# A chunk's residual sum and norm taken in four separate items; key norms kept aside, gate logits scaled once per event, last gates' functions one item later

## What is computed

```python
x = _layernorm(x + _L0_ffn_ref(x, ...))            # the end of the routed feed-forward
q = _rmsnorm((x @ Wq).reshape(B, T, H, D), q_rms_w) # H = 16, D = 64
k = _rmsnorm((x @ Wk).reshape(B, T, H, D), k_rms_w)
v = (x @ Wv).reshape(B, T, H, D)
gate = softplus(einsum('bthd,hd->bht', k, u_n) / sqrt(D))
bias = -dist * omega_eff * gate                     # per key and head
scores = einsum('bihd,bjhd->bhij', q, k) / sqrt(D) + bias
```

## Time and profile before

| | us |
|---|---|
| median of three runs (lowest to highest) | 2246.51 (2245.86 to 2251.53) |
| profiled execution, device time | 2246.59 |
| profiled execution, span from first to last instruction | 2244.8 |
| PE busy | 2050.4 (91% of the span) |
| DVE busy | 1368.2 (61%) |
| ACT busy | 1151.4 (51%) |
| POOL busy | 843.5 (38%) |
| mean granted TensorE clock | 0.953 of 2.4 GHz |

### The profile page before, as it was taken

One profiled execution on the slowest core, in us unless ns is written; L12 is line 12 of the kernel. 1 busy time (PEld: TensorE's weight loads), 2 busy tenths in 40 slices (PEclk: granted clock), 3 DMA queues, 4 the chain that ended last, 5 costly groups with the idle time before them and its releaser, 6 DMA issues.

```text
span 2244.8 us, 34359 instructions
## 1 busy us (share of the span) xinstructions
PE 2050.4 (91%) x11728; PEld 1168.5 (52%) x11728; DVE 1368.2 (61%) x3345; ACT 1151.4 (51%) x1859; POOL 843.5 (38%) x544
## 2 busy tenths in 40 slices
PE   5799999998496888796999999999999999999998
PEld 2333333334395454453565656556665655655644
DVE  4788888884532878774666666666666654333311
ACT  2366666666353677673455555555555553223232
POOL 5000000001502345342677777777777773000000
PEclk8799999999598999995999999999999999999999
DMA  5233333113174779877577667776777687533300
GB/s 179 98 127 131 131 128 119 59 51 112 62 202 123 219 232 333 251 240 185 139 179 176 157 163 178 176 172 154 171 178 179 158 218 198 129 89 85 90 5 10
DMA packets 260300, 335.88 MB, mean 150 GB/s; under 512 B 22732, under 2 KB 181756, under 8 KB 259720
## 3 DMA queue, kind: packets, MB, share of 16 engines
q1 hardware_dynamic: 244824, 305.82, 50.6%
q0 software_dynamic: 7664, 24.39, 3.0%
q10 hardware_dynamic: 7640, 3.48, 0.5%
HBM read 193.69 MB, written 122.62 MB: 141 GB/s over the span
## 4 chain that ended last, share of the span: by engine, by line
PE 40%; issue 6%; DVE 4%; SPq 2%; DMA 1%; ACT 0%; DVEq 0%
PE ps L1287 10%; PE ps L956 6%; PE ps L940 6%; PE ps L909 6%; PE ps L941 5%; PE ps L1238 2%; DVE a1mx L1012 2%; PE ps L1298 1%; PE ps L1275 1%; PE ps L1276 1%; PE ps L943 1%; DVE a1mx L1008 1%; SPq L1162 1%; DMA a1FQ<-s_q 0%; DVE a1mx L1005 0%
## 5 line engine op out<-in xcount | busy, mean ns | idle before, releaser
L1123 POOL TENSOR_TENSOR a1sum<-a1sum,a1prob 128x1024 f32<-128x1024 f32 (+3 forms) x256 | 462.9, 1808 | 82.6 <-ACT a1prob L1066 50.5
L1066 ACT ACTIVATE a1prob<-ps 128x512 f32<-128x512 f32 (+2 forms) x640 | 328.0, 554 | 243.6 <-PE ps L943 211.9
L479 DVE TENSOR_REDUCE a0grid<-ps 128x8 f32<-128x1024 f32 x288 | 351.3, 1223 | 100.6 <-PE ps L351 63.1
L1005 DVE CUSTOM_DVE_ANT_0 ps<-ps,c_mask_ij 128x128 f32<-128x128 f32 x496 | 264.4, 551 | 193.9 <-issue 189.7
L580 ACT ACTIVATE a0prob<-ps 128x1024 f32<-128x1024 f32 x288 | 286.2, 1024 | 167.3 <-PE ps L377 110.5
L940 PE MATMUL ps<-a1QA,a1KA 69*128 69x512 f32 (+3 forms) x768 | 284.3, 378 | 4.6 <-DMA a1QA<-a1neg 4.6
L956 PE MATMUL ps<-a1prob,a1V 128*64 128x512 f32 (+3 forms) x1536 | 272.9, 498 | 3.9 <-ACT a1prob L1066 3.9
L941 PE MATMUL ps<-a1QB,a1KB 128*128 128x512 f32 (+3 forms) x768 | 263.1, 350 | 0.0
L909 PE MATMUL ps<-a1KA,a1QA 68*128 68x128 f32 x744 | 224.6, 381 | 4.3 <-DMA a1KA<-s_g 3.4
L956 PEld LDWEIGHTS ps<-a1prob,a1V 128*64 128x64 f32 x1536 | 102.7, 138 | 171.6 <-issue 138.1
L1008 DVE TENSOR_REDUCE a1mx<-ps 128x1 f32<-128x320 f32 x248 | 146.0, 589 | 70.1 <-PE ps L909 67.2
(11 more groups left out here) (267 smaller groups left out, 3163.1 us busy)
## 6 DMA issues: line engine op xcount, KB each, us to landing
a1FQ<-s_q SPq DMA_DIRECT2D x128, 256.0 KB, 7.9
a1KB<-s_k SPq DMA_DIRECT2D x128, 256.0 KB, 8.6
s_xs<-c_zero POOLq DMA_DIRECT2D x19, 1024.0 KB, 9.5
s_q<-mqkT SPq DMA_DIRECT2D x32, 512.0 KB, 4.4
s_v<-mv SPq DMA_DIRECT2D x32, 512.0 KB, 5.8
s_k<-a1KH SPq DMA_DIRECT2D x32, 512.0 KB, 4.9
s_k<-a1KL SPq DMA_DIRECT2D x32, 512.0 KB, 5.9
a1KA<-s_k SPq DMA_DIRECT2D x64, 256.0 KB
```

What stands on the lines that cost most here:

```text
L479: dve.tensor_reduce(grid[g % 2][:, :, a:b + 1:b - a], banks(("max", k)), axis=AX.X, op=ALU.max).then_inc(s1_free, 1)
L1005: dve.tensor_tensor_reduce(bank[:, 0:w], bank[:, 0:w], const["mask_ij"][:, BANK - w:BANK], 1.0, LOWEST, ALU.add, ALU.max, mx[:, x % 2, h, ...
L1066: act.activation(weights_of(g, u)[:, group[0]:group[-1] + 1, off:BANK], both(e, u, group), ACT.Exp).then_inc(weighed, 1)
L1123: pool.tensor_tensor(t[:, :, off:BANK], t[:, :, off:BANK], weights_of(g, u)[:, :, off:BANK], ALU.add).then_inc(summed, 1)
```

## The change

`join` is taken apart into `add_up` (the sum), `count` (bn_stats) and `moments` (bn_aggr). For a chunk c + 2 the sum now stands in item 8 and the statistics in item 11 of chunk c; the moments follow in item 2 and the norm in item 5 of chunk c + 1. Chunk 1 has sum, statistics and moments in item 2 of chunk 0. In `scale` the reciprocal of a key's norm is written to a new tensor `kss`, kept for all chunks, and no longer multiplied into `z` there; `gates_a` multiplies the event's whole `z` by it in one instruction, and waits for that. `count` waits for the statistics' earlier reading, `moments` for the norm before. On ScalarE the last event's `soften` moves from n = 96 to n = 97, behind the weighing of the last keys.

```diff
@@ -1498,7 +1498,8 @@
         EVENTS = {24: range(0, 2), 72: range(2, 6), 96: range(6, 8)}
         wide = TILES * max(len(cs) for cs in EVENTS.values())
         zabs, g, gj = own("zabs", [P, wide, heads]), own("g", [P, wide, heads]), own("gj", [P, wide, heads])
-        z = own("z", [P, steps, TILES, heads])
+
+        z, kss = own("z", [P, steps, TILES, heads]), own("kss", [P, steps, TILES, heads])
         aug, augT = own("aug", [P, wide, P // heads, heads], F32R), [own(f"augT{r}", [4 * heads, CHUNK]) for r in range(2)]
         warm = own("warm", [P, 1])
         tmp = sq[0]
@@ -2194,18 +2195,26 @@
 
             dve = nc.vector
 
-            def join(c):
+            def add_up(c):
 
                 dve.wait_ge(gathered[c % 2], 16 * TILES * (c // 2 + 1))
                 if c > 1:
                     dve.wait_ge(x2_full, c - 1)
                 dve.scalar_tensor_tensor(acc[c % 2][:, :, :], x1[:, c * TILES:(c + 1) * TILES, :], 2.0, yg[c % 2][:, :, :], ALU.mult, ALU.add).then_inc(added, 1)
+
+            def count(c):
+
                 dve.wait_ge(added, c + 1)
                 if c > 0:
-                    dve.wait_ge(x2_full, c)
+                    dve.wait_ge(counted2, 2 * c * TILES)
                 for t in range(TILES):
                     dve.bn_stats(st2[:, t, :], acc[c % 2][:, t, :]).then_inc(counted2, 1)
+
+            def moments(c):
+
                 dve.wait_ge(counted2, (2 * c + 1) * TILES)
+                if c > 0:
+                    dve.wait_ge(x2_full, c)
                 for t in range(TILES):
                     dve.bn_aggr(mv2[:, t, :], st2[:, t, :]).then_inc(counted2, 1)
 
@@ -2234,17 +2243,15 @@
                 (tile, kind), i = kinds(n), nth(n)
                 c, t = divmod(tile, TILES)
                 dve.wait_ge(rooted3, i + 1)
-                dve.reciprocal(ss[i % 2][:, :], ss[i % 2][:, :]).then_inc(ss_full, 1)
+                norms = kss[:, c, t, :] if kind == WK else ss[i % 2][:, :]
+                dve.reciprocal(norms, ss[i % 2][:, :]).then_inc(ss_full, 1)
                 dve.wait_ge(ss_full, i + 1)
                 if i >= 3:
                     a = n // 3 * 3 + kind
                     old = [m for m in range(n) if kinds(m)[1] != WV][-3]
                     dve.wait_ge(t_full, at["half", old, 1] + 1)
-                if kind == WK:
-                    dve.wait_ge(z_full, c + 1)
-                    dve.tensor_tensor(z[:, c, t, :], z[:, c, t, :], ss[i % 2][:, :], ALU.mult).then_inc(z_scaled, 1)
                 dve.tensor_tensor(qk[i % 3][:, :].rearrange("p (h d) -> p h d", d=dim), pair(n).rearrange("p (h d) -> p h d", d=dim),
-                                  ss[i % 2][:, :].unsqueeze(2).to_broadcast([P, heads, dim]), ALU.mult).then_inc(scaled, 1)
+                                  norms.unsqueeze(2).to_broadcast([P, heads, dim]), ALU.mult).then_inc(scaled, 1)
 
             def parts(k):
 
@@ -2255,7 +2262,11 @@
             def gates_a(k):
 
                 n, zs, za, _, _ = parts(k)
-                dve.wait_ge(z_scaled, (events[k][-1] + 1) * TILES)
+                cs = events[k]
+                dve.wait_ge(z_full, cs[-1] + 1)
+                dve.wait_ge(ss_full, 2 * TILES * (cs[-1] + 1))
+                dve.tensor_tensor(zs, zs, kss[:, cs[0]:cs[-1] + 1, :, :].rearrange("p c t h -> p (c t) h"), ALU.mult).then_inc(z_scaled, 1)
+                dve.wait_ge(z_scaled, k + 1)
                 if k > 0:
                     dve.wait_ge(gated, GSTEP * k)
                 dve.scalar_tensor_tensor(za, zs, -1.0, zs, ALU.mult, ALU.max).then_inc(gated, 1)
@@ -2314,16 +2325,23 @@
 
             GSTEP = 8
             dve.wait_ge(made, PREPARED)
-            join(0)
-            norm(0)
+            for part in (add_up, count, moments, norm):
+                part(0)
             for n in range(NI + TLAG):
                 if 1 <= n <= NI and kinds(n - 1)[1] != WV:
                     scale(n - 1)
                 if n < NI and kinds(n)[1] != WV:
                     reduce(n)
                 c, o = divmod(n, 12)
+                if n == 2:
+                    add_up(1)
+                    count(1)
                 if o == 2 and c + 1 < steps:
-                    join(c + 1)
+                    moments(c + 1)
+                if o == 8 and c + 2 < steps:
+                    add_up(c + 2)
+                if o == 11 and c + 2 < steps:
+                    count(c + 2)
                 if o == 5 and c + 1 < steps:
                     norm(c + 1)
                 if n in EVENTS:
@@ -2437,8 +2455,9 @@
                     keep_x(c + 1)
                 if o == 11 and c + 1 < steps:
                     keep_z(c + 1)
-                if n in EVENTS:
-                    soften(event_of[EVENTS[n][0]])
+                for m, cs in EVENTS.items():
+                    if n == m + (cs[-1] == steps - 1):
+                        soften(event_of[cs[0]])
                 if n in split_at:
                     split(split_at.index(n))
                 for c in turn_gates.get(n, ()):
```

## The result

The changed kernel takes 2221.6 us in the median (2219.41 to 2230.44) beside 2246.9 (2245.86 to 2252.29) of the kernel before on the same chip: a ratio of 0.9885, 95% interval 0.9856 to 0.9914, 25.3 us less. The profiled execution took 2221.2 us, its span is 2219.4. The forecast was 2229, with a range of 2212 to 2241.

A forecast was written before the change was run, and what follows sets the result against it. VectorE's order of work, with z held behind GpSimd's subtraction, was taken as the bound. Terms 1.6 + 1.1 + 2.5 + 0 + 6.6 + 2.5 + 2.9 = 17.2 us off 2246.59 gave 2229.4, range 2212 to 2241.

The forecast's parts named there:

- Bound and mechanism: Middle stage's last part: VectorE's order of work sets the time; PE waits 32.6 us for mqk, holding costs z 25 us.
- Norm held: Item 5: GpSimd's subtraction holds the norm's tensor_scalar, costing PE 3.0 us per plain chunk; likeliest case, 2229 us, chance 0.48.
- X: Time by which a moved VectorE part ends after mqk of the keys; 4.3 us for the held norm.
- the prediction's rule: Value items: a part ending X us after mqk of the keys costs PE X - 1.2, leaving 0.4 of lateness.
- the floor: TensorE's minimum for a chunk of twelve items without idle gaps: 29.0 us.
- Add_up and count: Items 8 and 11: the sum, held by a subtraction, costs PE 0.6 us; the unheld bn_stats cost 0.2.
- the slack of 0.4: Value items, read from an undisturbed tile: 0.4 us more beyond VectorE's 0.8 us of idle before PE is late.
- Clock: Plain chunks: half of the half-clock loss seen behind 2.37 us of PE idling, charged at 0.9 us per chunk.
- a plain chunk: Norm 3.0, add_up 0.6, count 0.2 and clock 0.9 put such a chunk 4.7 us over the floor.
- no gain: Chunks 3 and 4: 10.8 us over the floor now, 2 x 4.7 then, each lower about 1.2 us more.
- handed back elsewhere: Rival: the gain is lost to DMA limits in chunks 2 to 5 or GpSimd behind key stores; 2245 us, chance 0.09.
- End of the stage: Weighing the last keys before the gates' functions moves everything up to the barrier 2.9 us earlier.

The follow-up runs named there:

- z alone: Kernel before with only the key norms kept aside and z multiplied once per event, join whole in item 2: ratio 0.9912, 17.4 us less in the medians.
- the join alone: Kernel before with only the join split into four items, z left in place: ratio 0.9969, 5.9 us less in the medians.
- functions back: Changed kernel with the last event's soften at n = 96 again: chunks unchanged, first maximum 8.30 us behind the last item's product.
- the last version: Changed kernel with norm in item 6, gathers one per tile, fifteen next-stage loads issued later: 2217.25 us beside 2230.32 of the changed kernel.

## Why the prediction was right, and where it was not

*Bound and mechanism.* Right: VectorE's order set this part outside chunks 3 and 4, and the holds on z were the largest piece. In the chunks z alone gives 15.3 us, the join alone 4.9, and both together ("functions back") 19.9. That the single gains add up is chance: in chunk 5 they make 13.5 where both together give 8.4, and in chunks 3 and 4 they lengthen by 4.5 and 2.3 where both together lengthen by 2.3.

*Norm held.* The mechanism was right, in chunks 1, 3 and 5 with 2.4 to 2.5 us; chunks 0 and 4 saw 1.0, chunks 2 and 6 none. The Trainium skill, "SBUF — State Buffer", section "Who interferes with whom", says of the shared pair of ports that "whoever issues first gets the shared pair for the whole instruction; the other **fully blocks**"; the trace agrees, down to the first of the four tensor_scalar, which starts at 769.99 ahead of the subtraction and is not held. The size was wrong: X, the time by which the norm ends behind the scaling of the keys, was put at 4.3 and is 3.27 (769.99 + 3.16 - 769.88). GpSimd's cast starts 5.6 us behind item 4's product, where 6.2 were taken: the first gather, 1.26 us beside the old sum, takes 0.99 without it, and the weighed keys, which came last there, by 0.29, no longer do. The remaining 0.4 is in the tensor_scalar behind the hold, which end 0.5 us after it, not 0.9. By the prediction's rule PE should lose X - 1.2 = 2.07; chunk 1 lies 1.9 over the floor. So the rule holds, and its input was 1 us too large. (The floor of 29.0 was a little low itself: in the last version chunk 1 takes 29.27 us with PE busy for 29.15.)

*Add_up and count.* Put at 0.6 and 0.2, they cost nothing in chunk 1: from 776.66 to 784.71 TensorE has no idle place of over 0.1 us. add_up was held as said (1.69 us, put at 1.73), but items 8 and 11 carry extra work of TensorE, the transposes of x (0.66 us at 776.16) and the gate products, which give VectorE more room. The step that failed is the slack of 0.4, read off a tile of the last chunk, which has neither. count was unheld as said.

*Clock.* 0.9 us per chunk was charged for the lower clock behind the norm's gap. The granted clock stayed 1.00 in chunks 1 and 5: behind the norm PE idled 1.41 us at a stretch (until 776.16), not 2.37. Behind 2.67 us of idle, in the experiment with the sum in item 5, the lower clock came.

With these three terms a plain chunk lies 1.9 us over the floor in place of 4.7, which is chunk 1's 3.9 us of gain in place of 1.1, and would be most of what chunks 0 (3.1 for 1.6) and 5 (8.4 for 6.6) gave beyond their terms. In chunks 2 and 6, where the norm met no subtraction, the gain was 4.2 and 3.6 for 2.5 each; the wide multiplication of z took 0.28 and 0.41 us there, near the 0.4 estimated, and 1.36 in the covered place at the end.

*Chunks 3 and 4.* Here the prediction was wrong by its own words: "wrong if [...] chunks 3 and 4 lengthen", and they lengthened, by 2.3 us. The step that failed is "no gain". Its own terms, 2 x 4.7 for the norm and its company and 2 x 1.2 for the two `lower`, make 11.8, already 1.0 more than the 10.8 of before; and the DMA share of 1.08 was taken only as a ceiling on the gain. With the plain chunk's measured 1.9 the same terms would make 6.2 over the floor; measured are 13.2, so some 7 us are another term. It is the transfers, which SyncE issues in order, the stores behind loads that nobody needs yet: with thirteen loads out of the way the two chunks lie 6.2 over the floor, 6.9 us less than in the changed kernel and 4.6 less than before. That the lengthening itself is handed-back time is argued: PE comes to these chunks 11 us earlier, and 0.6 MB more moved in them, 1.9 us at 331 GB/s. The rival "handed back elsewhere" named the place and the means; it was not a rival but a term of every case. The held sum of chunk 4 (1.48 us) and the first `lower` (3.36) were not tried apart. But the key split that `lower` met there was late itself, as GpSimd had waited 7.31 us for a store of keys; with thirteen loads moved this `lower` took 1.21 us.

*End of the stage.* Put at 2.9, measured 2.85 at the first maximum. Cause and size were right.

*Sum.* 17.2 was forecast; 20.9 in the chunks and 2.85 at the end were found, 23.8. The chunks other than 3 and 4 gave 9.0 more than their terms (the norm at two thirds of its price, no cost of the sum and the statistics, no lower clock), and chunks 3 and 4 took 2.3 back. So the mechanism of the likeliest case came true; that the time came out only 7 us under the forecast is in part luck, as two errors of opposite sign met. The other 1.6 us of the 25.4 between the two profiled executions are scatter: 2.0 us less lie ahead of the first product (723.40 and 721.44), 0.7 less between the first maximum and the next stage's start, and 1.1 more behind it. From that start to the end, where this change alters nothing, the traces of all versions here take 1199.7 to 1213.7 us.

## What to carry to other kernels

Before a part is moved into a slack, read the slack in the item where it will stand: items of the same kind that differ by 0.7 us of TensorE's work turned a cost into nothing here. A VectorE instruction that can be held behind GpSimd belongs where GpSimd's previous instruction has ended, and what makes GpSimd late (here four gathers in a row) is as good a lever as the instruction itself. Where a DMA share is near 1 on an in-order issuing queue, look for transfers that nobody waits for yet, standing ahead of stores that free a buffer: moving 3.5 MB of them alone gave 6.9 us in two chunks, and 4 MB, together with the norm and the gathers, 11.0.

## What the runs showed of the hardware

- A group of short VectorE instructions loses to GpSimd between two of its members: in chunk 1 the first of four tensor_scalar ran, the second was held to the end of the subtraction and took 2.38 us, the last two were not held.
- Issuing a DMA kept SyncE for 0.36 to 3.35 us in this part, and what stands behind it in its list is late by as much: the store of v in chunk 3 was issued 11.5 us after its values were ready (822.13 to 833.65). What makes one issue long is not shown.
- With all the loads in place chunks 3 and 4 moved 322 to 336 GB/s and took 68.8 to 73.3 us, whatever the order of VectorE's work, in nine traces. With eight to fifteen loads moved away, in four traces, two of them with the norm and the gathers moved as well, it was 308 to 317 GB/s, and 69.0 to 60.5 us.
